# Attention with slots: carried products and masked scores times slots on 64 array columns per head, and the scaled result turned in place of 1/z

## The reference

```
z = jax.lax.cumlogsumexp(s, axis=2)
g = jnp.exp(jnp.concatenate([z[:, :, :1], z[:, :, :-1]], axis=2) - z)
p = jnp.exp(s - z)
hk = hk * g_t[:, :, None, :] + k_t[..., None] * p_t[:, :, None, :]
okT = jnp.einsum('bhk,bhkm->bhm', q_t, hk)          # per token
pvT = jax.nn.softmax(okT, axis=-1)
hv = hv * g_t[..., None] + p_t[..., None] * v_t[:, :, None, :]
ovT = jnp.einsum('bhm,bhmv->bhv', pv_t, hv)         # per token
```

## Time and profile before

| | |
|---|---|
| median of 3 runs | 1313.72 us (1313.54 to 1313.87) |
| the profiled execution's own time | 1313.55 us |
| its span in the trace | 1311.8 us |
| PE busy | 1302.4 us, 99% |
| PE weight loads busy | 1150.9 us, 88% |
| DVE, ACT, POOL busy | 934.9, 535.4, 425.9 us |
| granted TensorE clock | 0.999 |

### The profile page before, as it was taken

The page is one execution under the profiler, slowest core; times in us unless marked ns, Lnnn a source line. Parts: engine busy times, 40 slices in busy tenths (PEclk is TensorE's granted clock), DMA queues, the critical chain, the costliest instruction groups (busy, mean ns, idle before and its releaser), DMA issues.

```text
span 1311.8 us, 21997 instructions
## 1 busy us (share of the span) xinstructions
PE 1302.4 (99%) x8652; PEld 1150.9 (88%) x8652; DVE 934.9 (71%) x1887; ACT 535.4 (41%) x1551; POOL 425.9 (32%) x390
## 2 busy tenths in 40 slices
PE   8999999999999999999999999999999999999998
PEld 7888888888888888888888988888888888988886
DVE  5777777777777777777777777777777777766654
ACT  5634443344334443444335434444334434632221
POOL 3412342254223431234125422343133413442211
PEclk9999999999999999999999999999999999999999
DMA  6002100010000100010001000010000110000000
GB/s 232 33 33 81 33 17 1 1 55 10 10 1 25 33 17 1 25 33 17 1 1 49 9 17 1 24 33 17 1 24 26 65 34 1 1 0 33 33 32 33
DMA packets 33847, 36.04 MB, mean 27 GB/s; under 512 B 3536, under 2 KB 24016, under 8 KB 33744
## 3 DMA queue, kind: packets, MB, share of 16 engines
q1 hardware_dynamic: 33744, 34.64, 8.3%
HBM read 30.43 MB, written 4.19 MB: 26 GB/s over the span
## 4 chain that ended last, share of the span: by engine, by line
PE 98%; DVE 0%; DMA 0%; issue 0%; ACT 0%; SPq 0%; POOLq 0%; POOL 0%; DVEq 0%
PE p L1062 15%; PE p L1063 15%; PE p L1064 15%; PE t L1120 5%; PE o L1304 3%; PE s L1188 3%; PE xb L1257 3%; PE p L1188 2%; PE o L1242 2%; PE o L1240 2%; PE t L1304 2%; PE s L1131 2%; PE s L1613 2%; PE s L1132 2%; PE s L1133 2%; PE s L1615 2%
## 5 line engine op out<-in xcount | busy, mean ns | idle before, releaser
L1062 PE MATMUL p<-wvg_hi,xt_hi 128*128 128x512 f32 x508 | 201.5, 397 | 0.0
L1063 PE MATMUL p<-wvg_lo,xt_hi 128*128 128x512 f32 x508 | 198.5, 391 | 0.0
L1064 PE MATMUL p<-wvg_hi,xt_lo 128*128 128x512 f32 x508 | 197.9, 390 | 0.0
L558 POOL TENSOR_TENSOR orstd<-ovar,minus_half 128x8 f32<-128x8 f32 x32 | 52.4, 1638 | 424.4 <-DVE ovar L1013 424.4
L520 POOL TENSOR_TENSOR s_lo<-sums,s_hi 128x512 fp32r<-128x512 f32 x64 | 83.1, 1299 | 225.5 <-ACT s_hi L649 225.5
L1062 PE MATMUL p<-xt_hi,wsqk_hi 128*128 128x512 f32 x372 | 147.9, 397 | 0.0
L1063 PE MATMUL p<-xt_lo,wsqk_hi 128*128 128x512 f32 x372 | 145.4, 391 | 0.0
L1064 PE MATMUL p<-xt_hi,wsqk_lo 128*128 128x512 f32 x372 | 145.1, 390 | 0.0
L624 ACT ACTIVATE v_tok<-p 128x256 f32<-128x256 f32 x128 | 49.6, 388 | 220.2 <-PE p L1064 216.3
L911 DVE COPY hv<-xb 64x128 f32<-64x128 f32 x192 | 55.1, 287 | 88.9 <-PE xb L1257 87.6
L1064 PEld LDWEIGHTS p<-wvg_hi,xt_lo 128*128 128x128 f32 x508 | 95.4, 188 | 20.7
(11 more groups left out here) (284 smaller groups left out, 3555.4 us busy)
## 6 DMA issues: line engine op xcount, KB each, us to landing
raw<-in_L_attn_Wv SPq DMA_DIRECT2D x32, 128.0 KB, 2.3
raw<-in_L_attn_Wg SPq DMA_DIRECT2D x32, 128.0 KB, 2.9
raw<-in_L_attn_Wo SPq DMA_DIRECT2D x16, 256.0 KB, 3.0
acc<-in_L_attn_hidden_states SPq DMA_DIRECT2D x4, 1024.0 KB, 5.6
out<-acc SPq DMA_DIRECT2D x16, 256.0 KB, 2.0
acc<-in_turned SPq DMA_DIRECT2D x3, 1024.0 KB, 8.6
raw<-in_L_attn_Ws SPq DMA_DIRECT2D x8, 256.0 KB, 2.8
raw<-in_L_attn_Wq SPq DMA_DIRECT2D x8, 256.0 KB, 3.0
```

What stands on the lines that cost most here:

```text
L558: nc.gpsimd.tensor_tensor(orstd[:], ovar[:], minus_half[:], ALU.pow).then_inc(orstd_done, 1)
L1062: nc.tensor.matmul(out_, lh, rh, start=(k == 0), stop=False)
L1063: nc.tensor.matmul(out_, lh, rl, start=False, stop=False)
L1064: last = nc.tensor.matmul(out_, ll, rh, start=False, stop=(k == n - 1))
```

## The change

- **Carried keys.** One product of 128 x 128 under a mask becomes two of 64 x 64, one for each head, each on 64 array columns. `XB` is set to zero once, since the other blocks are no longer written.
- **Scores times slots.** The result is computed turned (slots on the partitions, tokens along the bank). A chunk has two products on 64 array columns, with the slots as weights, and, for chunks 1 to 3, one product of the carried keys with all of q.
- **1/z.** It is no longer transposed: `okt` = result times `rz_t` is formed in the turned layout, transposed by TensorE, and read by VectorE in `OK_BANK`. The second factor 1/z is multiplied in after the transposes of the softmax numerator.
- **Carried values.** Three fp32r passes of 128 x 256 become two f32 products on 64 array columns. The high and low parts of the values and slots are gone, and ScalarE in place of VectorE copies the sums to `hv`.
- **Order.** The carried values of chunk 0 and 1 now stand among the scores times slots, and `running_keys(2)` waits until ScalarE has copied the values of chunk 0 out of the same bank.

```diff
@@ cell_scalar
+        def keep_values(act, cell, c):
+            act.wait_ge(hv_summed, cell.count(CH - 1, c + 1))
+            nc.scalar.activation(hv[:, c, :], XB[:, P:P + VW], ACT.Copy).then_inc(hv_kept, 1)
...
-            act.wait_ge(rz_turned, cell.count(1, 1))
-            nc.scalar.activation(rz_tok[:].rearrange("p c n -> p (c n)"), RZ_BANK[:], ACT.Copy).then_inc(rz_tok_done, 1)
-
             if not first(cell):
                 y_high(act, cell, 0)
+            keep_values(act, cell, 0)
+            if not first(cell):
                 y_high(act, cell, 1)
                 sums_high(act, cell, 0)
-                act.wait_ge(ok_summed, cell.count(1, 1))
-                slots_high(act)
-                values_high(act, cell, 0)
-            values_high(act, cell, 1)
+            keep_values(act, cell, 1)
...
-            act.wait_ge(pz_turned, cell.count(1, 1))
-            nc.scalar.activation(pz_t[:], PZ_BANK[:], ACT.Copy).then_inc(pz_t_done, 1)
@@ cell_vector
             dve.wait_ge(ok_summed, cell.count(1, 1))
-            dve.wait_ge(rz_tok_done, cell.count(1, 1))
-            nc.vector.tensor_tensor(flat, OB[:], rz_tok[:].rearrange("p c n -> p (c n)"),
-                                    ALU.mult).then_inc(ok_scaled, 1)
...
+            dve.wait_ge(rz_done, cell.count(1, 1))
+            nc.vector.tensor_tensor(okt[:], OB[:], rz_t[:], ALU.mult).then_inc(ok_scaled, 1)
...
+            dve.wait_ge(pz_turned, cell.count(1, 1))
+            nc.vector.tensor_tensor(pz_t[:], PZ_BANK[:], rz_t[:], ALU.mult).then_inc(pz_t_done, 1)
@@ cell_tensor
-                nc.tensor.matmul(XB[:, 0:P], k_tok[:, c, :], e_tok[:, c, 1:3, :].rearrange("p h m -> p (h m)"),
-                                 start=(c == 0), stop=True, skip_group_check=True).then_inc(hk_summed, 1)
+                for h in range(2):
+                    mm = nc.tensor.matmul(XB[h * DK:(h + 1) * DK, h * M:(h + 1) * M], k_tok[:, c, h * DK:(h + 1) * DK],
+                                          e_tok[:, c, 1 + h, :], start=(c == 0), stop=True, skip_group_check=True)
+                mm.then_inc(hk_summed, 1)
+
+            def running_values(c):
+                pe.wait_ge(v_done, cell.count(CH, c + 1))
+                pe.wait_ge(hk_kept, cell.count(CH - 1, min(c + 2, CH - 1)))
+                if c > 0:
+                    pe.wait_ge(hv_kept, cell.count(CH - 1, c))
+                for h in range(2):
+                    mm = nc.tensor.matmul(XB[h * M:(h + 1) * M, P + h * DV:P + (h + 1) * DV], e_tok[:, c, 1 + h, :],
+                                          v_tok[:, c, h * DV:(h + 1) * DV], start=False, stop=True, skip_group_check=True)
+                mm.then_inc(hv_summed, 1)
...
             for c in range(CH):
...
+                for h in range(2):
+                    nc.tensor.matmul(OB[h * M:(h + 1) * M, tokens(c)], e_tok[:, c, 1 + h, :], ws_t[:, c, h, :],
+                                     start=(c == 0), stop=True, skip_group_check=True)
+            running_values(0)
+            for c in (1, 2):
+                pe.wait_ge(hk_kept, cell.count(CH - 1, c))
+                nc.tensor.matmul(OB[:, tokens(c)], hk[:, c - 1, :], q_t[:, tokens(c)], start=False, stop=True,
+                                 skip_group_check=True)
+            pe.wait_ge(hv_kept, cell.count(CH - 1, 1))
+            running_keys(2)
+            pe.wait_ge(hk_kept, cell.count(CH - 1, CH - 1))
+            mm = nc.tensor.matmul(OB[:, tokens(CH - 1)], hk[:, CH - 2, :], q_t[:, tokens(CH - 1)], start=False, stop=True,
+                                  skip_group_check=True)
             mm.then_inc(ok_summed, 1)
+            running_values(1)
```

More of the change, by code:

```diff
@@ L304, in attention @@
         th = sb("th", [P, 2, VW])
[L305 to L311, removed]
+        hv = sb("hv", [P, CH - 1, VW])
         y = sb("y", [P, CH, 2, DV])
@@ L325, in attention @@
         pz_t = sb("pz_t", [P, T])
-        rz_t = sb("rz_t", [P, T])
-        sb("rest", [P, CH * DV])
+        sb("rest", [P, 2 * CH * DV])
         ws_t = sb("ws_t", [P, CH, 2, P])
@@ L531, in cell_gpsimd @@
                 sums_low(pool, cell.shifted(-1), 0)
[L533 to L542, removed]
+                sums_low(pool, cell.shifted(-1), 1)
             if last:
@@ L708, in cell_scalar @@
             values_scalar(act, cell, 2)
[L709 removed]
             values_scalar(act, cell, 3)
[L711 to L712 removed]
+            keep_values(act, cell, 2)
             if wo_J == 0:
@@ L905, in cell_vector @@
                 y_vector(dve, cell.shifted(-1))
[L907 to L912, removed]
             def keep_keys(c):
@@ L932, in cell_vector @@
             dve.wait_ge(ok_summed, cell.count(1, 1))
-            dve.wait_ge(rz_tok_done, cell.count(1, 1))
-            nc.vector.tensor_tensor(flat, OB[:], rz_tok[:].rearrange("p c n -> p (c n)"),
-                                    ALU.mult).then_inc(ok_scaled, 1)
[L936 to L939, removed]
+            dve.wait_ge(rz_done, cell.count(1, 1))
+            nc.vector.tensor_tensor(okt[:], OB[:], rz_t[:], ALU.mult).then_inc(ok_scaled, 1)
             if not first(cell):
                 y_sums(dve, cell, 1)
+                add_m24(dve, cell, 0)
+            dve.wait_ge(ok_turned, cell.count(1, 1))
+            by_token = OK_BANK[:].rearrange("p (g m) -> p g m", m=M)
+            nc.vector.tensor_reduce(top[:], by_token, AX_X, ALU.max).then_inc(top_done, 1)
             dve.wait_ge(top_done, cell.count(1, 1))
-            nc.vector.tensor_tensor(groups, groups,
+            nc.vector.tensor_tensor(groups, by_token,
                                     top[:].rearrange("p (g a) -> p g a", a=1).broadcast_to([P, 2 * CH, M]),
@@ L982, in cell_vector @@
                 car.norm1_tile(dve, 0, 1)
-            if first(cell):
-                slots_vector(dve, nxt)
-                keep_values(2)
-                sums_vector(dve, nxt)
-                inverse_vector(dve, nxt)
-            else:
-                keep_values(2)
             if last:
                 car.x_low(dve, 0, 0, X1[0])
-            elif not first(cell):
+            else:
                 slots_vector(dve, nxt)
@@ L1221, in cell_tensor @@
             running_keys(0)
-            pe.wait_ge(rz_done, cell.count(1, 1))
-            turned(RZ_BANK, [rz_t[:, tokens(c)] for c in range(CH)], rz_turned)
             if not first(cell):
                 turned_y(pe, cell, 0)
+                turned_y(pe, cell, 1)
             running_keys(1)
@@ L1230, in cell_tensor @@
             for c in range(CH):
-                if c == 2 and not first(cell):
-                    pe.wait_ge(rz_tok_done, cell.count(1, 1))
-                    turned_y(pe, cell, 1)
-                if c == 2:
-                    running_keys(2)
-                o = OB[:, c * P:(c + 1) * P]
-                if c > 0:
-                    pe.wait_ge(hk_kept, cell.count(CH - 1, c))
-                    nc.tensor.matmul(o, q_t[:, tokens(c)], hk[:, c - 1, :], start=True, stop=False)
-                nc.tensor.matmul(o.rearrange("p (h m) -> p h m", h=2), ws_t[:, c, 0, :], e_tok[:, c, 1:4:2, :],
-                                 start=(c == 0), stop=False)
@@ L1261, in cell_tensor @@
+                pe.wait_ge(s_summed, cell.shifted(-1).count(8, 4))
+            pe.wait_ge(ok_scaled, cell.count(1, 1))
+            turned(OK_BANK, [okt[:, tokens(c)] for c in range(CH)], ok_turned)
             token_proj(pe, cell, 2)
-            running_values(0)
             if not first(cell):
@@ L1265, in cell_tensor @@
             token_proj(pe, cell, 3)
-            running_values(1)
             if not first(cell):
                 rows_third(pe, cell)
-            pe.wait_ge(pz_done, cell.count(1, 1))
-            turned(PZ_BANK, [pz[:, c, :, :].rearrange("p h m -> p (h m)") for c in range(CH)], pz_turned)
+            pe.wait_ge(exp_done, cell.count(1, 1))
+            turned(PZ_BANK, [ok[:, c, :, :].rearrange("p h m -> p (h m)") for c in range(CH)], pz_turned)
+            running_values(2)
             if not last:
                 feature_proj(pe, nxt, 0, s_proj)
-                running_values(2)
                 feature_proj(pe, nxt, 1, q_proj)
```

51 lines of the change are left out of this document (11 added, 40 removed).

## The result

| | before | changed |
|---|---|---|
| median | 1313.8 us (4 runs, 1313.54 to 1313.92) | 1332.04 us (4 runs, 1331.81 to 1333.06) |
| ratio to before | | 1.014, 95% interval 1.0127 to 1.0153 |
| span of the profiled execution | 1311.8 us | 1330.2 us |
| PE, PE weight loads busy | 1302.4, 1150.9 us | 1305.6, 1103.8 us |
| DVE, ACT, POOL busy | 934.9, 535.4, 425.9 us | 867.6, 488.8, 312.4 us |

The changed kernel is 18.2 us slower. Every other engine has less to do, and the time is longer.

The account below looks back on a forecast made before the run. TensorE (PE), busy 99% of the span, was taken to bound the kernel. Per cell, products -1.27, ten column changes +2.00 and a wait +0.45 made +1.18 us, +38 us over 32 cells: 1351 us, range 1300 to 1367.

Parts of the forecast that it names:

- the ten changes: Ways into and out of five groups of 64-column products per cell, at 0.20 us each: 2.0 us a cell.
- the three pairs of carried keys: Carried-key products on 64 columns, each pair taken at 0.22 us: three times a cell, 0.66 us.
- The bound: Whole kernel: PE busy 99% of the span, so only TensorE's work and waits in its stream move the time.
- I price them by the nearest, those on 64 rows: 64-column products: two side by side for the price of one, so eight scores products cost 0.88 us a cell.
- The rival without overlap: 64-column pairs do not overlap: scores 1.76 and values 1.32 us a cell, 1401 us; chance 0.12.
- the low bound: Carried keys at 0.11 us a pair, since they move only 64 columns; products then save 1.60 us a cell.
- The wait at keys 2: TensorE waits for VectorE's masked copy before the last product with q: 0.45 us new per cell.
- The hidden wait on ScalarE's copy: running_keys(2) waits for the copy of values 0: 0.96 us, covered by 1.06 us of TensorE work.
- The sum: Per cell -1.27 + 2.00 + 0.45 = +1.18 us; by 32 cells +38 us, giving 1351 us.
- The low corner: Column changes at 0.15 us, keys at 0.11 a pair, wait 0.61: +0.5 us a cell and 1330 us.
- The free rival: Column changes cost nothing and waits eat most of the gain: -0.3 us a cell, 1304 us; chance 0.22.

Follow-up runs that it names:

- one_group: Kernel before with scores times slots and carried keys 1 and 2 on 64 columns in one stretch, first-cell x splits after okt scaling: 1301.41 us, ratio 0.9906.
- keys_alone: Kernel before with only the carried keys changed, to two 64 x 64 products on 64 array columns in their old places: 1335.01 us, ratio 1.0162.
- values_alone: Kernel before with only the carried values changed, to two f32 products on 64 array columns for three fp32r passes: 1331.37 us, ratio 1.0133.
- split_group: Changed kernel with chunk 1's q product with the carried keys moved between the scores of chunks 1 and 2, two more column changes: 1347.57 us, ratio 1.0258.
- filled_wait_m24: Changed kernel with y's second turn behind keys 2 and VectorE's first output-product addition ahead of the sums of y's second half: 1319.88 us, ratio 1.0042.
- both_waits_gone: Changed kernel with y's second turn behind keys 2, VectorE's output-product addition earlier, and first-cell x splits after okt scaling: 1314.62 us, ratio 1.0006.

## Why the prediction was right in direction and wrong in size

Two terms of the sum failed: the ten changes, priced at 2.00 us a cell, cost 1.7, and the three pairs of carried keys, priced at 0.66, cost 0.34. Together that is 0.62 of the 1.18 us a cell, 20 us of the 38. A cost that the sum did not have, in the first cell, hid part of this.

- **The bound.** Right. Less work on DVE, ACT and POOL (67, 47 and 114 us) gave nothing.
- **"I price them by the nearest, those on 64 rows".** Right: 0.88 us for eight products. The rival without overlap falls.
- **The carried keys at 0.22 us a pair.** Mis-sized: 0.11 to 0.12 (one_group). I had an average spacing of records from longer products (0.055 us) and took it for a floor; here four records take 0.11 to 0.12 together. Three pairs a cell, 0.32 us too much, 10 us in all. It was the low bound that was right.
- **Ten changes "at 0.20 us each".** Mis-sized: 0.15 into a stretch, 0.15 out of it into transposes and 0.20 into other products. The nine crossings that no wait covers sum to 1.5 us; with the tenth at 0.20 it is 1.7, so that 0.3 us a cell were too much, another 10 us. The mechanism, that a change of array columns costs what a change of rows costs, is shown by keys_alone, values_alone and split_group. The Trainium skill's page "TensorEngine Tiling (Array Packing)", Key Properties, says that a change of tiling mode drains the TensorE; these traces agree in that every change cost 0.15 to 0.20 us, with the weight loads idle and no releaser. A drain itself is in no row, so that the reason stays an interpretation.
- **The wait at keys 2, 0.45 us.** The number is right, filling it freed 0.43 (filled_wait_m24), but by luck. I had 0.87 us from the start of keys 2 to the product behind the copy, with 0.22 for the keys. In the chain above it is 0.75: 1.14 us from 603.84 to 604.98, less 0.17 for the way in and 0.22 for the product itself. The keys take 0.12 of it. Both figures were too large by about 0.1 us, and what is left between them, way out and wait, was not. With my 0.87 and the true price of the pair the wait would have come out at 0.56. The hidden wait on ScalarE's copy was hidden, and came out when split_group took away its cover.
- **The sum.** With the two corrections it is -1.60 + 1.70 + 0.45 = +0.55 us a cell; measured are 0.43 to 0.44. Of the 0.1 us between, 0.06 stands in the kernel before, where the first L1131 behind the carried values takes 0.18 us in the chain and the next ones 0.12; the rest is not traced. The low corner, +0.5 us a cell and 1330 us, comes close to the 1332 measured, but in part by chance: it had changes at 0.15 against a wait of 0.61, and nothing for the first cell.
- **What I had not seen.** The first cell. There the output product that hides `okt` is missing, and VectorE has the splits of x ahead of it. Taking the splits away from there gave back 3.9 us, 2.5 of waiting and about 1.4 by the lower clock, so that this cost made up part of what the sum had too much. In both_waits_gone the first cell still has three waits of 0.4 us, for two copies of keys and for `okt`, with no y to turn and no output product between; from its first stretch on 64 rows to the next it takes 27.7 us, against 26.8 before.
- **The free rival.** Its claim that the waits eat most of the gain was true in part; both_waits_gone shows the rest, that with these waits gone the crossings eat the whole saving of the pairs.

## What to carry to other kernels

Products on part of the array's columns are worth as much as those on part of its rows, half the time for a pair, but here each way into or out of such a stretch cost 0.15 to 0.20 us: count stretches before products, and use them only where several stand together (four pairs of scores won, single pairs of keys or values lost). When a result is needed one product later through another engine's copy, put work between, and follow the chain again after each move: here a set of transposes moved behind the scores came back as a wait on a bank three steps on. Look at the first and last passes of a loop apart from the steady ones; their cover is often missing.

## What the runs showed of the hardware

- Going from products on 128 array columns to products on 64 cost 0.15 to 0.17 us, and going back 0.15 into transposes and 0.20 into other products, with the weight loads idle for 0.17 us or 0.35 and no releaser; between 128 and 64 rows it was 0.20, with 0.35 idle.
- Two products on 64 columns each, on the same 128 rows, ran for the price of one on all columns: eight in 0.88 us.
- Four records of 64 x 64 f32 products took 0.11 to 0.12 us together, 0.03 us each.
- In one idle stretch of 2.9 us on TensorE the granted clock fell to its lower level; it was back 2.9 us after the work began again in the changed kernel, and 5.3 us after it in filled_wait_m24. Idle stretches of 0.4 us had no such fall.
